# Delta-rule attention with a routed feed-forward: beta's product in another PSUM bank and slot, k's scale split off from v's, k' ahead of the residual

## The reference

```python
x1 = x + attn(layernorm(x));  out = x1 + experts(layernorm(x1))
# attn, per row t and head
k = (x @ Wk) * rsqrt(sum(k*k) + 1e-12);  q = (x @ Wq) * SCALE
beta = sigmoid(x @ Wb)
S = S + k (beta * (v - k^T S))^T;  o = q^T S
o = o * rsqrt(mean(o*o) + EPS) * norm_w * silu(x @ Wg);  attn = o @ Wo
# experts: sum over the two chosen e of gate_e * gelu(x1n @ w1[e].T) @ w2[e].T
```

## Time and profile before

| | us |
|---|---|
| median of three runs | 909.89 |
| the profiled execution's own time | 914.49 |
| its span (first to last instruction) | 912.7 |
| TensorE busy | 850.3 (93%) |
| VectorE busy | 625.5 (69%) |
| ScalarE busy | 596.5 (65%) |
| GpSimd busy | 439.3 (48%) |
| kscale on GpSimd, 32 instructions | 52.7 |

### The profile page before, as it was taken

One profiled execution on the slowest core, in us unless ns is written; L12 is line 12 of the kernel. 1 busy time (PEld: TensorE's weight loads), 2 busy tenths in 40 slices (PEclk: granted clock), 3 DMA queues, 4 the chain that ended last, 5 costly groups with the idle time before them and its releaser, 6 DMA issues.

```text
span 912.7 us, 29508 instructions
## 1 busy us (share of the span) xinstructions
PE 850.3 (93%) x9870; PEld 669.4 (73%) x9871; DVE 625.5 (69%) x1832; ACT 596.5 (65%) x1645; POOL 439.3 (48%) x430
## 2 busy tenths in 40 slices
PE   3799999999999999999988979999999999999995
PEld 2578887788877888778876657777777777777773
DVE  4678898898988989888885755544455554455552
ACT  3478887888888888888766725444446544444551
POOL 2155554767677676676646543332223222222333
PEclk8999999999999999999997989999999999999998
DMA  6022222333233332332233252322233332223223
GB/s 225 2 71 66 82 65 77 95 95 106 84 95 99 90 107 83 97 99 82 84 107 88 72 118 48 48 48 48 43 48 66 50 50 46 46 46 46 47 36 34
DMA packets 50652, 67.14 MB, mean 74 GB/s; under 512 B 6464, under 2 KB 35008, under 8 KB 50528
## 3 DMA queue, kind: packets, MB, share of 16 engines
q1 hardware_dynamic: 36640, 46.46, 17.5%
q0 software_dynamic: 13344, 17.97, 11.5%
q10 hardware_dynamic: 544, 1.05, 0.3%
HBM read 41.84 MB, written 23.61 MB: 72 GB/s over the span
## 4 chain that ended last, share of the span: by engine, by line
PE 77%; issue 7%; ACT 4%; DVE 4%; POOL 4%; DMA 3%; SPq 0%; DVEq 0%; ACTq 0%; POOLq 0%
PE ps L1158 71%; DMA wst<-w 2%; PE ps L1247 2%; PE ps L1533 2%; ACT inverse_levels L789 1%; PE ps L1190 1%; PE ps L1413 1%; POOL kscale L616 1%; DVE inverse_levels L1815 1%; DMA wb_in<-wb 1%; POOL out L769 1%; POOL w_lo L665 0%; PE ps L1445 0%; ACT kq_wvg L844 0%; ACT Lh L789 0%
## 5 line engine op out<-in xcount | busy, mean ns | idle before, releaser
L789 ACT ACTIVATE inverse_levels<-ps 128x512 f16<-128x512 f32 (+1 forms) x324 | 163.0, 520 | 147.9 <-PE ps L1533 120.6
L769 POOL DMA_INDIRECT out<-inverse_levels,yidx x71 | 119.6, 1684 | 256.2 <-DVE inverse_levels L2273 194.6
L1158 PE MATMUL ps<-inverse_levels,w_hi 128*128 128x256 f16 (+1 forms) x1376 | 192.9, 255 | 1.9 <-issue 1.3
L2236 DVE SCALAR_TENSOR_TENSOR KpAT<-kq_wvg,inverse_levels 128x512 f16<-128x512 f32 (+1 forms) x144 | 98.5, 687 | 111.9 <-ACT inverse_levels L789 109.2
L1158 PE MATMUL ps<-inverse_levels,w_lo 128*128 128x256 f16 (+1 forms) x688 | 164.2, 255 | 0.0
L1158 PE MATMUL ps<-w_s,inverse_levels 128*128 x426 | 141.9, 379 | 6.5 <-issue 3.3
L1158 PEld LDWEIGHTS ps<-inverse_levels,w_hi 128*128 x1376 | 125.4, 98 | 15.7 <-issue 3.2
L1055 ACT ACTIVATE kq_wvg<-ps 128x512 f32<-128x512 f32 (+1 forms) x144 | 85.0, 590 | 67.0 <-PE ps L1158 51.1
L1158 PE MATMUL ps<-w_s,KpAT 128*128 x426 | 116.1, 273 | 1.0 <-issue 1.0
L789 ACT ACTIVATE inverse_levels<-kq_wvg 128x512 f16<-128x512 f32 (+1 forms) x144 | 89.8, 624 | 4.6
L1815 DVE CAST_PREDICATED inverse_levels<-mask_s,ps 128x256 f16<-128x256 int8 x192 | 82.1, 428 | 15.0 <-PE ps L1158 10.0
(11 more groups left out here) (239 smaller groups left out, 1920.7 us busy)
## 6 DMA issues: line engine op xcount, KB each, us to landing
wst<-w SPq DMA_DIRECT2D x58, 256.0 KB, 2.8
inverse_levels<-eye SPq DMA_DIRECT2D x35, 256.0 KB, 5.2
x_s<-x SPq DMA_DIRECT2D x32, 128.0 KB
out<-x_s SPq DMA_DIRECT2D x32, 128.0 KB, 1.7
x_s<-routed_rows SPq DMA_DIRECT2D x7, 260.0 KB
Lh<-routed_rows SPq DMA_DIRECT2D x7, 260.0 KB
Vp<-routed_rows SPq DMA_DIRECT2D x7, 260.0 KB
rowA<-routed_rows SPq DMA_DIRECT2D x7, 260.0 KB
```

The source lines that it names most:

```text
L769: pool.indirect_dma_start(out=out, out_offset=bass.IndirectOffsetOnAxis(ap=yidx[:, q, a:a + 1], axis=0), in_=yrow[:, q % 2, a, :], in_offs ...
L789: return act.activation(dst, src, ACT.Copy, scale=scale)
L1158: return pe.matmul(dst, lhsT, rhs, start=start, stop=stop, **kw)
L2236: dve.scalar_tensor_tensor(hlo[:, q % 2, two, 0:n], hf[:, m, :].rearrange("p (m n) -> p m n", m=2)[:, :, 0:n], H_SCALE, hhi[:, q % 2, two, ...
```

## The change

Five edits. `p_beta` lies in bank 6 (columns 256 to 259), where the second half of the Gram products is, and no longer in bank 7. `beta_proj` stands directly behind `k_proj`'s second half. `beta_exp` stands ahead of `k_square`. GpSimd raises k's 4 arguments first, with `s_kscale`, and v's 4 arguments in an instruction of its own, with the new semaphore `s_vscale`. `k_prime` stands ahead of `attention_residual`. The waits follow: the Gram's second half and `rank` now wait for beta's exponential, `beta_proj` waits for the masked scores of the tile before, `v_gate` and the next `k_norm` wait for v's scale.

```diff
-        p_beta = PS[7][:, 0:H]
+        p_beta = PS[6][:, 256:256 + H]
...
-                rsqrt(kscale[:, n % 2, :], karg[:, :], 2 * H).then_inc(s_kscale, 1)
+                rsqrt(kscale[:, n % 2, 0:H], karg[:, 0:H], H).then_inc(s_kscale, 1)
+                rsqrt(kscale[:, n % 2, H:2 * H], karg[:, H:2 * H], H).then_inc(s_vscale, 1)
...
+                beta_exp(i - 2)
                 k_square(i - 2)
-                beta_exp(i - 2)
...
-                done(pe, s_oTl, n - 3)
-                done(pe, s_lg, n - 4)
-                if not XR <= n < T - XR:
-                    done(pe, s_xn2Ts, n - 4)
-                    done(pe, s_xnTl, n)
-                    done(pe, s_res, n - 4)
+                done(pe, s_AT, n - 1)
+                if n == 0:
+                    pe.wait_ge(s_wsl, 2)
...
                 if a == 1:
+                    done(pe, s_eb, n)
...
                 done(pe, s_AT, n + RANK_AFTER)
+                done(pe, s_eb, n + RANK_AFTER + 1)
...
                 k_proj(i - 1, 1)
+                beta_proj(i - 1)
                 x_make(i - 2, 1)
...
                 q_proj(i - 1, 1)
-                beta_proj(i - 1)
                 x_make(i - 3, 6)
...
-                done(dve, s_kscale, n - 1)
+                done(dve, s_vscale, n - 1)
...
                 done(dve, s_th, n)
+                done(dve, s_vscale, n)
...
                 y_masked(i - 4, 3)
+                k_prime(i - 3)
                 attention_residual(i - 6)
-                k_prime(i - 3)
```

More of the change, by code:

```diff
@@ L303, in build @@
         s_kscale = sem("k_scale_ready")
+        s_vscale = sem("v_scale_ready")
         s_kp = sem("kprime_ready")
@@ L1072, in _ @@
             state_hi(T - 4)
+            beta_exp(T - 1)
             k_square(T - 1)
-            beta_exp(T - 1)
             q_evac(T - 1)
```

## The result

The changed kernel takes 917.43 us (median of four runs, 915.47 to 919.24) against 909.63 us of the kernel before (four runs, 906.01 to 910.32). The ratio is 1.0097, 95% interval 1.0076 to 1.0117. It is slower by 7.8 us. I forecast slower by 17.4 us: the direction and the place were right, the size was twice too large.

A forecast was written before the change was run, and what follows sets the result against it. TensorE looked like the bound, but at level 3 a chain through ScalarE, TensorE and VectorE and the residual's wait set the pace. 0.62 + 0.05 us per tile times 28, less 1.4, added to 909.9 gave 927.3 us; range 915 to 932.

The forecast's parts named there:

- The swap: VectorE, k' ahead of the residual: the residual and the xnT_make waiting for it come 0.72 us later per tile.
- the rule in both halves: Skill's rule on VectorE: next operation starts only when the pipe is empty; a semaphore costs nothing extra. Forecast rejected both.
- k_transposes: TensorE's k_transposes, waiting for k': with k' done long before, its wait of 0.10 us per tile goes.
- Beta's product: TensorE's six matmuls, moved earlier, no longer precede level 1's x_make: 0.05 us more per tile on the chain to level 3.
- The split power: GpSimd, two 4-column powers for one of 8: k's scale ready 0.5 us early, 0.39 us more GpSimd time, no effect.
- The sum: Attention stage: 0.67 us per tile times 28 is 18.8 us, less 1.4, so 17.4 us slower.
- The first tiles: Tiles 0 to 2, VectorE waiting for k's scale: gains 0.63, 0.27 and 0.27 us; with the last tile 1.4 together.
- Absorbed in part: Rival: xnT_make stalls, but later gaps ahead of y_make and o's transposes shrink; 0.38 us per tile, 919 us; chance 0.13.
- Faster: Rival: the residual isn't what holds xnT_make, so k' first gains 4 to 11 us, say 903 us; chance 0.09.
- Nothing comes of it: Rival: the stall at xnT_make comes, but gains and absorption together equal it; 1 us, so 911 us; chance 0.08.

The follow-up runs named there:

- e2: Changed kernel with the residual put back ahead of k', all other edits kept: 911.2 us, 0.9939 of the kernel before; timed again on another chip 900.47 us, 0.9904.
- e9: Kernel before with only beta's edits (bank, place, waits and exponential): 912.13 us, ratio 0.9958.
- e10: Kernel before with only GpSimd's 8-column power split into two of 4 columns, k's first: 912.68 us, ratio 0.9966.
- e8: Kernel before with the split power and k' ahead of the residual, without beta's edits: 926.01 us, ratio 1.0091.
- e13: Kernel before, unchanged, profiled once more: 914.11 us, no stretch at the lower clock in the steady tiles, 27 steps together 384.7 us.
- e1: Kernel before with only k' moved ahead of the residual, power still over 8 columns: 944.55 us, ratio 1.0307.

## Why the prediction was right in direction and wrong in size

**The swap, forecast 0.72 us per tile at `xnT_make` (bounds 0.61 and 0.72): measured 0.60.** The mechanism held to the letter: 27 waits, 14.0 us, `xnT_make` 0.06 us behind the residual. The step that failed is "I take 0.72, since the longer step belongs to k' wherever it stands". The longer step of 0.45 us belonged to no instruction and to no number of semaphores. It was k' waiting for GpSimd. With the split the wait is gone, and k' follows by 0.34 us behind a 0.42 us operation like any other; the residual follows it by 0.60 us. Over 28 tiles the 0.12 us too much are 3.4 us.

This also corrects my use of the Trainium skill, "VectorE: DVE Perf Modes", section "The DRAIN you can't avoid". I wrote that the trace speaks against the rule in both halves. On the first half I left out how the section goes on: "A next op that is not held starts earlier". In the trace the residual starts 0.60 us behind the start of a k' of 0.68 us, so the record of one operation overlaps that of the next by 0.08 us. That shows that k' doesn't cost its whole recorded time in front of the residual; whether the pipe was empty when the residual started, these records don't tell, and no run here has an operation that is held. For the second half, that a semaphore costs nothing extra, the trace agrees: in the changed kernel k' waits for several semaphores that were raised long ago, and starts as soon as its neighbours do.

**k_transposes, forecast -0.10 us: measured -0.17 in the changed kernel.** Its distance to `xnT_make` falls from a median of 0.80 to 0.62 us. I credited it to the swap. Most of it was to be had without: 0.80 goes to 0.69 us in `e2`, `e9` and `e10` alike, by ending the same wait of k' for GpSimd, and only the other 0.06 us are the swap's. Over 28 tiles the 0.07 us too little are 2.0 us.

**Beta's product, forecast +0.05 us on the chain (bounds 0 and 0.16): measured +0.04 to +0.08.** By the medians of the tiles, `x_make` at level 3 stands 13.05 us behind the last `k_transposes` in `e8`, which has all but beta's edits, and 13.13 and 13.08 us in the two profiles of the changed kernel. Against the kernel before (13.01 to 13.04) it would be 0.04 to 0.12, but that comparison can't be put down to beta's product: with the split alone the distance is 13.11 us too.

**The split power, forecast nothing in the steady tiles: wrong.** "ahead of where k' can now start, with 0.5 us to spare" is right for the changed kernel (0.43 us measured). The error is that I never asked it of the kernel before, where the same sum gives nothing to spare: 220.31 against 220.43. It was an edit that takes a wait away, and I priced it as one that only adds GpSimd time.

**The sum.** With 0.60 - 0.17 + 0.08 = 0.51 us per tile from the medians, 27 steps would add 13.8 us, where 28 x 0.67 = 18.8 was forecast. The profiles without a stretch at the lower clock have sums of 397.4 us after and 384.7 us before (`e13`), which is 12.7 us or 0.47 per tile. So of the 6.1 us between 18.8 and 12.7, some 4.5 are the terms above (3.4 for the swap and 2.0 for `k_transposes`, less 0.8 for beta's product), 0.5 are the 28th tile, and 1.1 lie in tiles that differ from the median one, which I haven't taken apart. The first tiles were forecast right: tile 4 starts 1.5 us sooner (61.6, 60.3 and 62.5 us in the three profiles with split and swap, 63.0 on average in the five of the kernel before), where I had worked out 1.2.

That leaves 12.7 - 1.5 = 11.2 us, or 1.2%. The measured 0.97% and 0.95% (8.8 and 8.7 us) are 2.4 us below, and the difference of the medians, 7.8 us, 3.4 us. This last part of the miss belongs to no term of the forecast that the runs could name. It is the size of one or two stretches at the lower clock (16.02 - 14.16 = 1.9 us for the one shown), and the kernel before had 6 in 5 profiles; but with the counts above it is not shown that they are the reason.

The rivals. *Absorbed in part* came nearest with its 919 us, by luck: it had the same stall at `xnT_make`, less gaps that would shrink on the way from `k_transposes` to the next `x_make` at level 3, and that distance did not shrink (13.02 us before, 13.05 in `e8`, 13.10 after). *Faster*, by which the swap gains by itself, is refuted by `e1` and by the 27 waits for the residual. *Nothing comes of it* is refuted by the interval, which begins at 1.0076.

## What to carry to other kernels

If an instruction follows its neighbour later than others of the same size do, subtract the ends of all its inputs before calling it overhead: here k' started a constant 0.13 us behind GpSimd's power over 25 tiles, while no wait was listed. Ask each question of slack for the kernel before as well as for the one after. And when two results feed two places in another engine's list, fix both orders together: the matched pairs gave 0.994, the crossed ones 1.001 and 1.010.

## What was not expected of the hardware

A short wait can hide under the instruction in front. With its scale ready, k' starts 0.34 us behind the start of the residual, 0.08 us before that one's recorded end of 0.42 us; waiting, it started at 0.45 us. So only 0.00 to 0.04 us of this wait showed as idle time of VectorE in the kernel before, and no list of waits had it. GpSimd's power costs 1.65 us for 8 columns and 1.98 to 1.99 us for two of 4, where the earlier trace rows had let me expect 2.04. The same program takes 4.6 us of "issue" idling, some 7.5 us in all, at the start of the expert stage in most profiles and none in a few. Stretches at TensorE's lower clock, which make a step 1.7 to 3.2 us longer, fall on some tiles of some executions, in the case shown right behind 3.5 us in which TensorE was busy for 2.50.
